# The last add of a quaternion product moves from VectorE into an accumulating TensorE transform, and every engine's order is written out

## The reference

```python
def _to_quaternion(x):
    p1 = jnp.diff(x, axis=1, prepend=x[:, :1])
    p2 = jnp.roll(x, 1, axis=2)
    p3 = jnp.cos(x)
    return jnp.stack([x, p1, p2, p3], axis=-1)
...
def _attention(x, aw, ab, pw, pb):
    ...
    q, k, v = jnp.split(qkv, 3, axis=-1)
    qk = _hamilton(_to_quaternion(q), _to_quaternion(k))
    qkv_p = _hamilton(qk, _to_quaternion(v))
    f = jnp.fft.fftn(qkv_p.astype(jnp.complex64), axes=(-3, -2))
    out = jnp.fft.ifftn(f * _spectral_filter(S), axes=(-3, -2)).real
    a = out[..., 0] * (1.0 + 0.1 * _modulation(S))
    return a.reshape(B, S, E) @ pw + pb
```

## Time and profile before

| | before |
|---|---|
| three runs, median (lowest to highest) | 1503.81 us (1503.05 to 1507.08) |
| the profiled execution: time and span | 1503.8 us, the span from its first to its last instruction |
| busy: TensorE matmul | 1395.6 us (93%), 6198 instructions |
| busy: TensorE weight loads | 990.6 us (66%) |
| busy: VectorE | 1250.3 us (83%), 1511 instructions |
| busy: ScalarE | 1042.7 us (69%) |
| busy: POOL | 360.9 us (24%) |
| mean granted TensorE clock | 0.981 of 2.4 GHz |

### The profile page before, as it was taken

One profiled execution on the slowest core, in us unless ns is written; L12 is line 12 of the kernel. 1 busy time (PEld: TensorE's weight loads), 2 busy tenths in 40 slices (PEclk: granted clock), 3 DMA queues, 4 the chain that ended last, 5 costly groups with the idle time before them and its releaser, 6 DMA issues.

```text
span 1503.8 us, 20880 instructions
## 1 busy us (share of the span) xinstructions
PE 1395.6 (93%) x6198; PEld 990.6 (66%) x6198; DVE 1250.3 (83%) x1511; ACT 1042.7 (69%) x2411; POOL 360.9 (24%) x251
## 2 busy tenths in 40 slices
PE   6999999999899999899999899999889999999858
PEld 4677766666566666566665667656677677777636
DVE  3344467877999989999959897999999999999996
ACT  6455757676886777766877768777857787776652
POOL 0001203110221402011131411131543353344410
PEclk9999999999999999999999999999999999999989
DMA  7763445335544554533363335355555556555244
GB/s 270 261 255 139 157 146 185 118 114 168 167 135 148 179 164 135 206 117 111 109 216 113 99 107 168 121 155 174 162 184 167 158 176 198 162 174 160 86 112 155
DMA packets 111243, 238.02 MB, mean 158 GB/s; under 512 B 13207, under 2 KB 52844, under 8 KB 109644
## 3 DMA queue, kind: packets, MB, share of 16 engines
q1 hardware_dynamic: 106588, 227.31, 47.9%
q0 software_dynamic: 4544, 9.38, 1.8%
HBM read 185.59 MB, written 43.86 MB: 153 GB/s over the span
## 4 chain that ended last, share of the span: by engine, by line
PE 44%; issue 20%; DVE 16%; ACT 9%; POOL 8%; DMA 2%; SPq 0%; ACTq 0%; POOLq 0%; DVEq 0%
PE bank L1363 8%; PE bank L1351 7%; PE bank L1353 6%; PE bank L1352 6%; POOL RSTD L1025 4%; PE bank L1543 3%; DVE AM L1087 3%; POOL ytok L1040 3%; ACT ROWS L865 2%; PE bank L1458 2%; DVE SH L1217 2%; DVE TA L1083 2%; PE bank L1452 1%; ACT ROWS L878 1%; DVE TA L1092 1%
## 5 line engine op out<-in xcount | busy, mean ns | idle before, releaser
L1025 POOL TENSOR_TENSOR RSTD<-SS,power_half 128x4 f32<-128x4 f32 x96 | 158.8, 1654 | 816.7 <-ACT ROWS L865 816.5
L1363 PE MATMUL bank<-SH,WD 128*128 128x512 f32 x512 | 263.6, 596 | 0.8 <-DVE X L1233 0.8
L1351 PE MATMUL bank<-NH,GU 128*128 128x512 f32 x512 | 245.5, 479 | 2.0 <-DMA GU<-halves 1.0
L1217 DVE TENSOR_TENSOR SH<-SH,bank 128x512 f32<-128x512 f32 x256 | 172.4, 682 | 76.4 <-ACT SH L853 46.4
L1087 DVE TENSOR_TENSOR AM<-AM,TA 128x1024 f32<-128x1024 f32 x192 | 230.2, 1219 | 0.9
L1083 DVE TENSOR_TENSOR TA<-QKV 128x2048 f32<-128x2048 f32 x96 | 219.5, 2287 | 1.2
L1353 PE MATMUL bank<-NL,GU 128*128 128x512 f32 x512 | 203.0, 397 | 0.0
L1352 PE MATMUL bank<-NH,GU 128*128 128x512 f32 x512 | 202.6, 396 | 0.0
L853 ACT ACTIVATE SH<-bank 128x512 f32<-128x512 f32 x256 | 153.1, 605 | 59.6 <-PE bank L1353 57.5
L878 ACT ACTIVATE ROWS<-bank,RSTD 128x128 f32<-128x128 f32 x384 | 110.0, 374 | 56.2 <-POOL RSTD L1025 50.8
L1578 PE MATMUL bank<-XT,GU 128*128 128x256 f32 x624 | 147.5, 381 | 0.3 <-DVE SH L1335 0.3
(11 more groups left out here) (232 smaller groups left out, 2764.8 us busy)
## 6 DMA issues: line engine op xcount, KB each, us to landing
GU<-halves SPq DMA_DIRECT2D x112, 512.0 KB, 4.2
QKV<-QKV SPq DMA_DIRECT2D x32, 720.0 KB
GU<-in_w_gu SPq DMA_DIRECT2D x39, 512.0 KB, 3.6
xg<-in_c_fill SPq DMA_DIRECT2D x8, 2080.0 KB
WD<-in_w_d SPq DMA_DIRECT2D x128, 128.0 KB, 2.2
FC<-ready_w SPq DMA_DIRECT2D x32, 512.0 KB, 5.2
WQ<-ready_w SPq DMA_DIRECT2D x32, 384.0 KB, 4.8
WD<-in_w_d SPq DMA_DIRECT2D x39, 256.0 KB, 3.8
```

The costliest lines, as they stand in the source:

```text
L1025: pool.tensor_tensor(RSTD[:], SS[:], (power_one if k[0] == "at" else power_half)[:], ALU.pow).then_inc(power_done, 1)
L1217: dve.tensor_tensor(SH[:, g % 4, :], SH[:, g % 4, :], banks[2 + g % 2][:], ALU.mult).then_inc(h_ready, 1)
L1351: pe.matmul(out, w_hi, x_hi, start=True, stop=False)
L1363: pe.matmul(banks[4][:], WD1[:, slot, :], SH[:, g % 4, :], start=first, stop=last).then_inc(down_done, 1)
```

## The change

The fold keeps only its first instruction. TensorE transforms slice 0 and slice 3 of TA one after the other into the same bank, the second accumulating on the first. So TA is held until the transform is done: "ham" 1 waits for freq_done in place of the fold. XG is written by "gain" alone, which now waits for the previous projection.

The planner and its tuned numbers are gone. In their place stands a table, PLACES: for each step name and engine, the place of each key in that engine's order. schedule() reads the orders off it. Its orders hold the same steps as the planner's, but not at the same places: of TensorE's 969 steps 820 can be kept in their relative order, of VectorE's 1225, 919, of ScalarE's 1049, 813, of SP's 432, 313, of POOL's 246, 210. Most of the others move by one to three places. One count that a ScalarE wait is made from (sums_before) is now taken in VectorE's order, at "normed" of kind "at", instead of ScalarE's, at "scale".

```diff
-HAM, FOLD = 11, 2
+HAM = 11
...
-class Plan:
...
-TUNE = {
...
+PLACES = {
...
+    "fold": {
+        "DVE": (
+            137, 223, 344, 488, 178, 269, 384, 519, 310, 453, 591, 703, 419, 554, 676, 860, 633, 789, 914, 1041, 751, 947, 1073,
+            1164, 823, 979, 1105, 1185, 889, 1011, 1131, 1207,
+        ),
+    },
+    "freq": {
+        "PE": (
+            130, 200, 290, 392, 165, 240, 322, 416, 266, 368, 468, 552, 346, 440, 535, 678, 502, 621, 723, 833, 590, 749, 856,
+            933, 642, 775, 884, 944, 702, 803, 908, 957,
+        ),
+    },
...
 def schedule():
...
+    every, at = step_keys(), {}
+    for name, engines in PLACES.items():
+        for engine, places in engines.items():
+            mine = [key for key in every[name] if TAKES_PART.get((name, engine), lambda key: True)(key)]
+            assert len(mine) == len(places), (name, engine, len(mine), len(places))
+            for key, place in zip(mine, places):
+                at.setdefault(engine, {})[place] = (name, key)
+    orders = {engine: [steps[i] for i in sorted(steps)] for engine, steps in at.items()}
...
-    sums_before = count_before("ACT", ("keys_exp", "query"), lambda name, key: name == "scale" and key[0] == "at")
+    sums_before = count_before("DVE", ("keys_exp", "query"), lambda name, key: name == "normed" and key[0] == "at")
...
                 if i == 1:
-                    dve.wait_ge(fold_step, n * FOLD)
+                    dve.wait_ge(freq_done, n)
...
             elif name == "fold":
                 dve.wait_ge(ham, (n + 1) * HAM)
-                dve.tensor_tensor(pair(TA, 0, 3), pair(TA, 0, 3), pair(TA, 1, 2), ALU.subtract).then_inc(fold_step, 1)
-                dve.wait_ge(fold_step, n * FOLD + 1)
-                if earlier("fold", k):
-                    dve.wait_ge(proj_done, upto("proj", earlier("fold", k)))
-                dve.tensor_tensor(XG[:], TA[:, 0, :], TA[:, 3, :], ALU.add).then_inc(fold_step, 1)
+                dve.tensor_tensor(pair(TA, 0, 3), pair(TA, 0, 3), pair(TA, 1, 2), ALU.subtract).then_inc(folded, 1)
             elif name == "gain":
                 dve.wait_ge(gain_loaded, 16)
                 dve.wait_ge(freq_done, upto("freq", k))
+                if earlier("gain", k):
+                    dve.wait_ge(proj_done, upto("proj", earlier("gain", k)))
...
             elif name == "freq":
-                pe.wait_ge(fold_step, FOLD * upto("fold", k))
+                pe.wait_ge(folded, upto("fold", k))
                 bank_free(pe, 6, name, k)
-                pe.matmul(banks[6][:], hartley[:], XG[:], start=True, stop=True).then_inc(freq_done, 1)
+                pe.matmul(banks[6][:], hartley[:], TA[:, 0, :], start=True, stop=False)
+                pe.matmul(banks[6][:], hartley[:], TA[:, 3, :], start=False, stop=True).then_inc(freq_done, 1)
```

More of the change, by code:

```diff
@@ L161 @@
-TUNE = {
[L162 to L179, removed]
-}
@@ new lines, in schedule @@
+def schedule():
+    every, at = step_keys(), {}
[6 more added lines that the diff above has]
+    orders = {engine: [steps[i] for i in sorted(steps)] for engine, steps in at.items()}
+    assert all(sorted(steps) == list(range(len(steps))) for steps in at.values())
+    keys = {}
+    for name, engines in PLACES.items():
+        per_engine = [[key for n, key in orders[engine] if n == name] for engine in engines]
+        longest = max(per_engine, key=len)
+        if name == "normed":
+            longest = keys["turn"]
+        elif name == "route":
+            longest = [(t, i) for t, last in longest if last == 3 for i in range(4)]
+        assert all([key for key in longest if key in some] == some for some in per_engine), name
+        keys[name] = longest
+    halves, half_of = list(range(HALVES)), {}
+    freed = [key[0:2] for name, key in orders["DVE"] if name == "ham" and key[2] == HAM + 1]
+    for i, key in enumerate(key[0:2] for name, key in orders["ACT"] if name == "views" and key[2] == 0):
+        half_of[key] = i if i < HALVES else half_of[freed[i - HALVES]]
+    return orders, keys, half_of
@@ L553, in program @@
         sem(n) for n in ("turns_done", "diff_done", "rounded", "reduced", "cos_done"))
-    ham, fold_step, freq_done, gained, proj_done, proj_added = (
-        sem(n) for n in ("ham", "fold_step", "freq_done", "gained", "proj_done", "proj_added"))
+    ham, folded, freq_done, gained, proj_done, proj_added = (
+        sem(n) for n in ("ham", "folded", "freq_done", "gained", "proj_done", "proj_added"))
     fc_done, gelu_done, mp_done, mlp_added = (sem(n) for n in ("fc_done", "gelu_done", "mp_done", "mlp_added"))
```

547 lines of the change are left out of this document (364 added, 183 removed), and 128 rows, old and new, of the table PLACES.

## The result

The changed kernel takes 1532.96 us (median; 1531.86 to 1537.05), the one before 1504.67 us (1503.05 to 1507.08) in runs beside it: a ratio of 1.0185, 95% interval 1.0166 to 1.0204. It is slower by 28 us, where 1486 was forecast with a range of 1465 to 1505. It moved the other way, and out of the range.

The account below looks back on a forecast made before the run. TensorE was taken to bound the first stage, both engines nearly full in the second, VectorE fuller in the third. From 1503.8 us, +2.6 +1 -8 +1 +4 -7 -9 and -2 for clock gave 1486, range 1465 to 1505.

Parts of the forecast that it names:

- the edit by stage: Fold and transform: second matmul less VectorE's saved add, +2.6 us first stage, +1 second, -8 third and last.
- the places: The new table's engine orders: named holes -7 us, other holes -9, clock behind long filled holes -2.
- SP's queue: SP's reordered DMA issues: block-number load 32 places later, scatters and row stores shifted; charged nothing.
- Named holes: Three places in TensorE's order: start -1.7 us, 793 us -4, last chain's end -1.5; together taken as -7.
- unnamed: TensorE's other holes with more work ahead: some 33 us of filling, a quarter taken, -9 us, ends 0 and -25.
- clock: TensorE's clock behind other long holes that get filled: -2 us.
- the start's: At 15.86 us on TensorE, first expert step goes ahead of the second tile's centring: -1.7 us.
- At 793 us: TensorE's 3.30 us hole before a down projection, then clock 0.62; one expert step fills it: -4 us.
- A: Rival: TensorE becomes the bound and pays its added 27.5 us whole; 1523 us, chance 0.12.
- B: Rival: VectorE held at TA by a transform late behind experts, 12 to 14 us; 1500 us, chance 0.12.
- C: Rival: the new orders give nothing, the edit alone -1 us; 1503, or 1499 with some named fills; chance 0.14.
- D: Rival: TensorE has much room, added matmuls cost nothing, VectorE's 23.7 us come back whole; 1463 us, chance 0.14.

## Why the prediction was wrong

Two groups of terms failed: the edit by stage, and the places with SP's queue among them. In the orders that the changed kernel has, the edit was taken at +1 and costs 4 to 9 us; the places and SP's queue were taken at -18 and cost 19, the larger miss by far.

**The edit: the worth by stage.** The prediction took TensorE's 27.5 us as cheap: +2.6, +1 and -8 for the edit, with "TensorE's 11.2 more there go into its 25 us of idle time". Measured for the same terms, no hold and no order changed: +14 us (+20 for the matmuls, -7 for the add). The 25 us, and the 38 of the second stage, were not room. They are many short waits, for ScalarE's rows above all (37.8 us in the whole kernel, 12.3 in the second stage and 6.9 in the third, where VectorE's products for the routed experts make 7.1 more). With the second matmul unbusy time is 105.7 us for 108.2. Counting unbusy time said how much TensorE waits, not that anything could be put there. And VectorE's wait for the transform at the gain, charged with +4, grew by 18 us in that run; how much of the 20 us is that wait stays open. That VectorE was "the fuller one" in the third stage by 8 us was read as "the bound": its relief brought 7 of 16 us.

**The places.** Named holes -7, unnamed -9, clock -2, so -18. The table with the old fold is at +19, with both DMA issues moved at +9. Of the named holes, the start's was there (expert (0, 0) ends 2.8 us earlier), but in the four kernels that have the table's orders and the fill moved back, expert (0, 16) ends 1.1 to 2.5 us later than before. In the changed kernel itself it ends 4.1 us earlier, and the stall for WD follows. At 793 us the hole became two (the changed kernel's timeline has 1.61 us before 810.37 and 1.22 before 815.99; the window 808 to 818 shows a clock of 1.00 for the 0.62 of the earlier trace rows); in the kernel before, this move and that of the MP load do bring 6 us. At the end nothing came: transform, projection and centring stand in a row with waits of 1.21 and 0.94 us between them, and from the last transform's start to the last mproj matmuls it is 17.6 us before and 17.7 after.

For the unnamed ones the count was "45 of them have more work ahead", taken at a quarter; TensorE's unbusy time stayed as it was. Why is argued, not shown: a hole filled in the old timing is met by no work of the old timing once the order before it has shifted.

The -2 for the clock has no row behind it, and no run shows it: the mean granted clock is 0.981 before and 0.980 after, and in the last 87 us it is 0.82 to 0.86 in the kernels with the table's orders (0.90 in the changed kernel with both DMA issues moved) and 0.89 to 0.91 in those with the planner's (0.85 with the add on GpSimd).

Which of the many swaps cost the +9 stays open: in that kernel the mproj matmuls are later by 2.5 us at 1026 us, 8.9 at 1127, 7.9 at 1419 and 14.1 at 1458, so it comes in two stretches, and no single swap was tried in either. In the second the table issues the last two down projections of the routed experts one behind the other; the low clock is not all of it, since the changed kernel with both DMA moves loses the same 6 us there.

**SP's queue at nothing.** The prediction went through the block numbers, the scatters and the row stores and wrote "I charge nothing". It didn't list what lies next to what. Two fills in a row cost 7 to 8 us in three comparisons (3 to 7 by the profiled spans), and with the MP load the changed kernel loses 11 to 15 to them. That the two fills stand side by side was to be read from the orders; what it would cost was in no row.

**The sizes.** The forecast was -17 against the kernel before and the result +28, a miss of 45. The edit was taken at +1 (-4 for the work, +5 for the waits) and is +20 in the old orders; the orders were taken at -18 and are +19, of which DMA issues are 10; that is 19 + 37 = 56, and the two overlap by 11 (below).

**What held.** The durations: 0.86 us start to start for each of the two accumulating matmuls (1504.28 to 1505.14 for the last pair), VectorE's busy time and TensorE's to 3 us. The transform of (5,0) stands directly behind its fold (969.96 + 1.22, then 971.32), and no multiply waits for TA in the changed kernel. In the old orders that hold is 6.7 us of waits, just above the 0 to 5 allowed. The gain's waits are 7.8 us for the matmul and 12.5 "issue", 20.3 for the 12 or more forecast.

**The rivals.** A came nearest: the sum paid for the most part, 17 to 24 of 27.5, though through which queue is open. Its 1523 took the places as a gain of 12 and was still 10 too low. B's hold shows only in the old orders. C had the edit at -1; it is +14 to +20 in the old orders and +4 to +9 in the table's. D is refuted: weight loads are 66% of the span and the extra matmuls were paid. (The Trainium skill, Trainium Kernel Development and Optimization, on reading a trace, has the weight loads' busy share as a good measure of closeness to the limit. Read as room for more work, as the rival read it, it is contradicted by the run with the second matmul: by it a third of the array's time would have been free, and 20 of the 27.5 us were paid all the same.)

**The parts together.** The edit in the old orders is +20, the table with the old fold +19; both are +28, not +39. So the edit costs less in the table's orders: 9 us, 8 with the fill moved in both kernels and 4 with both DMA issues moved (19 - 11 and 13 - 9; 7, 5 and 1 by the profiled spans; the intervals of the last pair overlap, and the changed one of that pair ran at a clock of 0.982 to 0.988 for 0.979 to 0.983, so the 4 may be low). The table fits the edited fold: with the old one TensorE waits 5.7 us for the fold's add, with the new one 1.7, and nothing is held at TA. The whole stays behind the kernel before.

## What to carry to other kernels

When two engines are both busy for over nine tenths of a stage, their unbusy time doesn't say which one pays: add a known amount of work to one and take a known amount from the other, as here (+20 for 27.5 us on TensorE, -7 for 16 us on VectorE), before trading work between them, and put the added work where the other engine doesn't wait for it. When a change reorders queues, write down the DMA issues side by side with their sizes; one small load behind two large copies cost as much as all named holes were to bring. Moves in an order are worth testing a few at a time: one hole filled and one load moved gave 0.4%, the whole table took 0.6% even with its DMA issues put right.

## What the runs showed of the hardware

With two 2 MB copies issued in a row a 128 KB load behind them landed after 29.0 us and TensorE stood 9.0 us for it; with the same copies apart the worst was 17.0 and TensorE didn't wait for WD. Two accumulating fp32 matmuls of 512 columns start 0.86 us apart, as two separate ones do. A 128x512 fp32 add takes 1.54 us on GpSimd and 0.69 on VectorE; cut to 32 columns it still takes VectorE 0.19 us. The granted clock was 0.62 over the 8.5 us behind a hole of 3.30 us, and 1.00 over 10 us that held two of 1.61 and 1.22.
